# A new order of tiles, routing and quads, and up-projection weights of half 0 read from a ring that VectorE fills

## The reference

```python
x = x + _L0_conv_ref(_ln_c(x), conv_w_in, conv_w_out, conv_bin_weights)
t = _to_tokens(x)
t = t + _L0_ffn_ref(_ln_t(t), gate_w, gate_b, w1, w2, w3)
# _L0_ffn_ref: 16 experts, hidden width 128
logits = einsum('bsd,de->bse', x, gate_w) + gate_b
top_probs, top_idx = lax.top_k(softmax(logits), 2)
hidden = silu(einsum('bsd,edh->bseh', x, w1)) * einsum('bsd,edh->bseh', x, w2)
out = einsum('bseo,bse->bso', einsum('bseh,eho->bseo', hidden, w3), dispatch)
```

## Time and profile before

| | us |
|---|---|
| median of 3 runs | 467.33 (464.56 to 467.99) |
| the profiled execution | 460.52 |
| its span, first to last instruction | 458.7 |
| first sort of half 0 | 108.3 |
| first `up` of half 0 | 190.4 |
| last sort of half 1 | 263.3 |
| first `up` of half 1 | 309.0 |
| last `down` ends | 393.6 |

### The profile page before, as it was taken

One profiled execution on the slowest core, in us unless ns is written; L12 is line 12 of the kernel. 1 busy time (PEld: TensorE's weight loads), 2 busy tenths in 40 slices (PEclk: granted clock), 3 DMA queues, 4 the chain that ended last, 5 costly groups with the idle time before them and its releaser, 6 DMA issues.

```text
span 458.7 us, 8416 instructions
## 1 busy us (share of the span) xinstructions
PE 337.7 (74%) x2564; PEld 273.3 (60%) x2564; DVE 265.0 (58%) x576; ACT 224.3 (49%) x484; POOL 190.0 (41%) x165
## 2 busy tenths in 40 slices
PE   4676669854567743568887899978999999667665
PEld 4544448723455332457676797768778887555553
DVE  2958575879794576133333342203566662589995
ACT  4682745623567254444434444334555553256563
POOL 1187013402678235433333380007765400287770
PEclk9859785555555655555656669976999899555555
DMA  8999100000112104112222223342545432133321
GB/s 272 279 326 386 56 0 1 1 0 12 38 50 56 28 21 128 40 29 73 64 57 65 67 69 87 74 99 74 138 105 123 95 79 43 41 75 109 91 74 53
DMA packets 55388, 39.89 MB, mean 87 GB/s; under 512 B 37660, under 2 KB 49692, under 8 KB 54708
## 3 DMA queue, kind: packets, MB, share of 16 engines
q1 hardware_dynamic: 42804, 29.25, 22.5%
q0 software_dynamic: 12384, 10.10, 9.1%
q10 hardware_dynamic: 160, 0.01, 0.0%
HBM read 20.08 MB, written 19.14 MB: 85 GB/s over the span
## 4 chain that ended last, share of the span: by engine, by line
PE 49%; DVE 28%; issue 10%; ACT 6%; DMA 4%; POOL 2%; SPq 1%; DVEq 0%; ACTq 0%; POOLq 0%
PE banks L878 11%; PE banks L870 8%; PE banks L869 8%; PE banks L808 6%; PE banks L843 4%; DVE tok L1146 4%; DVE tok L1144 3%; DVE chosen L1210 2%; DVE cand L1204 2%; DMA xs<-sorted_y,back 2%; PE banks L891 2%; ACT xs L554 2%; PE banks L678 1%; ACT wcol L555 1%; DVE ct L966 1%
## 5 line engine op out<-in xcount | busy, mean ns | idle before, releaser
L1289 POOL DMA_INDIRECT sorted_x<-xs,addr x64 | 75.6, 1181 | 99.4 <-ACT xs L554 69.4
L1295 POOL DMA_INDIRECT xs<-sorted_y,back x64 | 75.0, 1172 | 97.1 <-issue 82.5
L1197 DVE SCALAR_TENSOR_TENSOR power<-banks,fold 128x512 f32<-128x512 f32 x46 | 31.8, 691 | 123.8 <-PE banks L870 107.9
L870 PE MATMUL banks<-shared,w_all 128*128 128x128 f16 x368 | 78.7, 255 | 0.0
L869 PE MATMUL banks<-shared,w_all 128*128 128x128 f16 x368 | 77.3, 255 | 0.1
L808 PE MATMUL banks<-shared,tok 128*76 128x131 f16 x256 | 40.0, 307 | 44.5 <-ACT wcol L555 25.1
L554 ACT CAST xs<-banks 76x512 f16<-76x512 f32 x64 | 37.2, 581 | 66.5 <-PE banks L808 66.1
L878 PE MATMUL banks<-w_all,power 128*128 x368 | 60.9, 318 | 4.6 <-ACT enh L593 2.1
L878 PEld LDWEIGHTS banks<-w_all,power 128*128 128x128 f32 x368 | 54.6, 228 | 10.2 <-issue 9.7
L808 PEld LDWEIGHTS banks<-shared,tok 128*76 128x76 f16 x256 | 27.4, 172 | 55.7 <-DVE tok L1146 40.4
L820 PE MATMUL banks<-ident,tok 128*76 128x128 f16 x256 | 40.3, 311 | 17.7 <-ACT w_raw L561 6.9
(11 more groups left out here) (175 smaller groups left out, 534.5 us busy)
## 6 DMA issues: line engine op xcount, KB each, us to landing
sorted_x<-zeros SPq DMA_DIRECT2D x2, 2944.0 KB, 30.8
w_raw<-sorted_x SPq DMA_DIRECT2D x22, 256.0 KB, 4.0
sorted_y<-filt SPq DMA_DIRECT2D x96, 32.0 KB
sorted_y<-enh SPq DMA_DIRECT2D x88, 32.0 KB, 1.8
w_raw<-in_L_ffn_w SPq DMA_DIRECT2D x5, 512.0 KB, 15.7
xs<-in_x SPq DMA_DIRECT2D x8, 256.0 KB, 5.3
out<-cen_sq SPq DMA_DIRECT2D x8, 256.0 KB, 2.7
shared<-in_t_fwd SPq DMA_DIRECT2D x1, 1024.0 KB, 8.0
```

The source lines that it names most:

```text
L870: last = nc.tensor.matmul(dst, of_expert(experts[(i % 2) * QUAD + b], a + 1, HID).bitcast(F16), tokens[:, b, :, :], start=False, stop=True)
L1289: nc.gpsimd.indirect_dma_start(out=sorted_x[k].rearrange("(g s) c -> g (s c)", s=GRP), out_offset=bass.IndirectOffsetOnAxis(ap=addr[:, k, ...
L1295: nc.gpsimd.indirect_dma_start(out=yl[m % YL_RING], out_offset=None, in_=sorted_y[k].rearrange("(g s) c -> g (s c)", s=GRP), in_offset=bas ...
```

## The change

Five edits go together.

1. On TensorE `places_for` is cut in three (`counts_for`, `ranks_for`, `places_for`), which for half 1 come at tiles 24, 27 and 29 instead of all at 26. VectorE does its part, `sort_places(1)`, after the last 0/1 matrix of half 0. `owners_of` is cut in `past_of` (tile 8) and the rest (tile 17); `owners_for(0)` comes at tile 8. ScalarE's `gap_exponential(1)` and the table load come after tile 24.
2. 4 tiles of half 1 are sorted up front instead of 8; the other 28 go into 19 quads instead of 24 into 12. Of a quad's tiles, one part is sorted between `up` and `down`, the other after the octet's transposes. VectorE writes the 0/1 matrices for quad q+1 ahead of `product(q)`.
3. The loop over quads is one loop over both halves: `down` of the last two quads of half 0 comes between the first `up`s of half 1. The transposes of an octet come after the `up` and `down` of the even quad before it.
4. In half 0 `up` reads its weights from a ring of four quads at fixed addresses. VectorE fills it two quads ahead with four copies a quad, 128x512 of 16 bits, whose source address is taken from a register. One extra matmul of 512 columns (`stay_warm`) stands ahead of each `up`. Half 1 and every `down` read through TensorE's registers as before.
5. The return of half 0 starts at quad 4 and takes 18 quads, instead of 3 and 16. `slot_weights(0)` moves into quad 2.

```diff
-OWNERS_AFTER, ROUTE_AFTER, PLACES_AFTER = 4, 14, 26
-UPFRONT, SORT_STEPS = 8, 12
+PAST_AFTER, OWNERS_AFTER, ROUTE_AFTER = 8, 17, 14
+COUNTS_AFTER, RANKS_AFTER, PLACES_AFTER = 24, 27, 29
+UPFRONT, SORT_STEPS = 4, 19
+FILLERS = 1
-RET_START, RET_STEPS, BACK_LAG = 3, 16, 3
+RET_START, RET_STEPS, BACK_LAG = 4, 18, 3
+FETCH_AHEAD, FETCH_RING = 2, 4
...
+            def up_weights(k, i, b, a, experts):
+                if k == 0:
+                    return fetched_w[:, (i % FETCH_RING) * QUAD + b, a * HID:(a + 1) * HID].bitcast(F16)
+                return of_expert(experts[(i % 2) * QUAD + b], a, HID).bitcast(F16)
+            def stay_warm(count, spare):
+                for _ in range(count):
+                    nc.tensor.matmul(spare, ident16[:, :], perm[:, 0:BLK], start=True, stop=True)
...
+                if k == 0:
+                    pe.wait_ge(fetched, q + 1)
...
+                    if a == 0 and k == 0:
+                        stay_warm(FILLERS, bank[first_bank + q % 2])
...
+            for q in range(HALVES * NQ + DOWN_LAG):
+                k, i = q // NQ, q % NQ
+                n = OCTETS * k + i // 2
+                first, second = halves_of(sorts_in(q))
+                if k < HALVES:
+                    up(k, i, experts[n])
+                for t in first:
+                    sort_tile(t)
+                if q >= DOWN_LAG:
+                    before = q - DOWN_LAG
+                    down(before, experts[OCTETS * (before // NQ) + before % NQ // 2])
+                if k < HALVES and i % 2 == 0 and n + 1 < HALVES * OCTETS:
+                    experts[n + 1] = owners(n + 1)
+                    transpose_tokens(n + 1)
+                for t in second:
+                    sort_tile(t)
...
+            def fetch(i):
+                o = i // 2
+                if i % 2 == 0:
+                    used = regs[o % 2][0:blocks_of(o)]
+                    nc.vector.load(used, owner[0:1, 0, o * OCT:o * OCT + len(used)])
+                    fetching[o] = [nc.vector.snap(r, min_val=0, max_val=E - 1) for r in used]
+                if i >= FETCH_RING:
+                    dve.wait_ge(h2_done, i - FETCH_RING + 1)
+                for b in range(QUAD):
+                    last = nc.vector.tensor_copy(fetched_w[:, (i % FETCH_RING) * QUAD + b, :],
+                                                 w_all[:, bass.ds(fetching[o][(i % 2) * QUAD + b], 1), 0:4 * HID].rearrange("p o n -> p (o n)"))
+                last.then_inc(fetched, 1)
...
+                    for n in sorts_in(q + 1):
+                        one_hots(n)
                     product(q)
                     if k == 0:
-                        for n in sorts_in(i):
-                            one_hots(n)
+                        if i + FETCH_AHEAD < NQ:
+                            fetch(i + FETCH_AHEAD)
+                        if i == 2:
+                            slot_weights(0)
```

More of the change, by code:

```diff
@@ L319, in build @@
         in_xg = [sem(f"in_xg{o}") for o in range(XG_RING)]
[L320 to L321 removed]
+        xt_ps, xt_done, h1_done, h2_done, silu_done, hid_done, y_ps, y_done, fetched = (
+            sem(n) for n in ("xt_ps", "xt_done", "h1_done", "h2_done", "silu_done", "hid_done", "y_ps", "y_done", "fetched"))
         y_stored = [sem(f"y_stored{r}") for r in range(YS_RING)]
@@ L358, in sorts_in, with halves_of @@
             left = HT - UPFRONT
-            return range(HT + UPFRONT + left * i // SORT_STEPS, HT + UPFRONT + left * (i + 1) // SORT_STEPS) if i < SORT_STEPS else ()
+            return range(HT + UPFRONT + left * i // SORT_STEPS, HT + UPFRONT + left * (i + 1) // SORT_STEPS) if i < SORT_STEPS else range(0)
+        def halves_of(tiles):
+            return tiles[0:len(tiles) // 2], tiles[len(tiles) // 2:]
         block = ctx.enter_context(nc.Block())
@@ L569, in _ @@
                 hott_out(t)
-                if t == PLACES_AFTER:
+                if t == COUNTS_AFTER:
                     gap_exponential(1)
@@ L606, in result @@
                                bank[OUT_BANKS[n % 2]].rearrange("p (k q x y) -> p k q x y", k=KT, q=2, y=16)).then_inc(res_done, 1)
[L608 to L617, removed]
-                        for n in sorts_in(i):
[L619 to L622, removed]
+            tokens_out(0)
+            for q in range(HALVES * NQ + DOWN_LAG):
+                k, i = q // NQ, q % NQ
+                first, second = halves_of(sorts_in(q))
+                if k < HALVES:
+                    gate(q)
+                for n in first:
+                    sorted_out(n)
+                if q >= DOWN_LAG:
+                    y_out(q - DOWN_LAG)
+                if k < HALVES and i % 2 == 0 and OCTETS * k + i // 2 + 1 < HALVES * OCTETS:
+                    tokens_out(OCTETS * k + i // 2 + 1)
+                for n in second:
+                    sorted_out(n)
+                if k == 1:
+                    for m in tiles_in(i, RET_START, RET_STEPS):
+                        high_part(m)
             for n in range(TURN):
@@ L759, in window, with counted, counts_for @@
                 return perm[:, at:at + count * HT]
-            def places_for(k):
+            misc = bank[MISC_BANK]
+            def counted(k):
+                return [groups[:, k, c:c + 1].to_broadcast([P, P]) for c in range(CHUNKS)]
+            def counts_for(k):
                 pe.wait_ge(chosen_done, k + 1)
@@ L773, in places_for, with ranks_for @@
                     nc.tensor.matmul(bank[0], below, chosen[:, k, j, :, :].rearrange("p e t -> p (e t)"), start=(j == 0), stop=False)
+            def ranks_for(k):
                 pe.wait_ge(groups_done, k + 1)
-                counted = [groups[:, k, c:c + 1].to_broadcast([P, P]) for c in range(CHUNKS)]
                 for c in range(CHUNKS):
@@ L1230, in return_end @@
                 add_tiles((HT * (k + 1)) // TURN - 1)
+            for i in range(FETCH_AHEAD):
+                fetch(i)
             for k in range(HALVES):
```

81 lines of the change are left out of this document (44 added, 37 removed).

## The result

| | before | after |
|---|---|---|
| median (us) | 465.94 (463.99 to 467.99) | 412.19 (410.25 to 415.43) |
| ratio | | 0.8853 [0.8779, 0.8926] |
| the profiled execution, its span | 460.52, 458.7 | 415.43, 413.4 |
| mean granted clock | 0.682 | 0.738 |

The account below looks back on a forecast made before the run. In half 0's sort quads no engine was full: short waits chained at a 0.59 clock. Savings of 15.0 (sort stage) and 28.9 (half 0), less 1.5 (half 1), made 42.4 off 460.5, or 418; forecast 421 us, range 405 to 446.

Parts of the forecast that it names:

- The sort stage: Before the first `up`: owners' wait gone, routing cut in three, fewer tiles up front; 15.0 us saved, `up` near 175.4.
- the table load: Sort stage: ScalarE's load of 1.28 us now stands between tiles that wait for ScalarE, costing about 1.1.
- What is late next: End of sort stage: the load of sorted slots starts near 168, lands near 172, just when TensorE needs it.
- The clock: Half 0: first four quads at the lower clock, 18.2 us, then the full clock with TensorE busy 3.2 of 3.7.
- VectorE's price: Half 0: VectorE needs 3.7 us a quad, copies 4 x 0.40 = 1.6 of it, and sets the pace at full clock.
- The range's lower end: Copies at 0.23 and a clock that rises at once: half 0 about 76, the time 404 to 411 us.
- The additions: End of half 0: GpSimd's eight additions fall beside the last copies and cost 4 us.
- one VectorE instruction among them took 2.80: Half 0's additions, seen in the profile before: they take 8.03 us, one VectorE instruction among them 2.80; 4 us allowed.
- The rival of copies behind GpSimd's scatters: Half 0: each copy waits about 1.0 us for GpSimd, 7.1 a quad, half 0 163, time 478 to 485; chance 0.04.
- Half 1: Keeps its registers; its 84.6 us grows by 1.5, since its first two quads now have a `down`; some 86.
- which its last gathers hide: Half 1: the return of half 0 is two steps later, and its last gathers were to hide that.
- The sum: Whole kernel: 15.0 + 28.9 - 1.5 = 42.4 us saved, 460.5 becomes 418; 421 forecast.

Follow-up runs that it names:

- the gathers apart: Against the kernel with GpSimd's additions behind the last copy: gathers two a quad from half 1's fifth quad, return one quad later; 397.91 us, ratio 0.8532.
- the late additions: Against the kernel after: GpSimd starts its eight additions only behind half 0's last VectorE copy; 403.88 us, ratio 0.8646; run again 408.44, 0.8715.

## Why the prediction was right, point by point

**The sort stage**, 15.0 forecast, 17.8 measured. Four of its mechanisms are in the rows: the owners without a wait, the routing as 6.2 us of TensorE's own work (1.1, 3.6 and 1.5 from the start of each piece, at 144.01, 150.55 and 156.19, to the next tile; the forecast had 6.5 ahead of the gaps that it fills), the table load (2.10 instead of 0.40: 1.7 where 1.1 was forecast), and VectorE late at the first tile of half 1 (2.50, forecast 3.2). What made up the 2.8 above the forecast was not taken apart; one part seen in the rows is the clock, which rose for some microseconds (1.04 instead of 1.91 for the same four matmuls).

**What is late next.** The slots' load went out at 165.42 and its transposes at 170.04 with 0.53 of idle time: in time, with nothing to spare, as forecast.

**The clock.** Right in kind and too cautious in size: forecast at the full clock from the fifth quad, 18.2 us for the first four; measured 11.0 (172.6 to 183.6), with the clock at full some 4 us behind the first `up`. The reason given, that the gaps of the sort's chain are loosened, is what the run without a ring bears out (15.0 us of waits for the sort before, none there). Which part of the new order did it was not told apart: the sorts between `up` and `down`, the matrices written ahead, or 28 tiles in 19 quads instead of 24 in 12. Against the forecast half 0 gained 7.2 by this term. One reading of the forecast's was wrong: the slice of 284 to 288, given as half 1, lies in half 0, in its quads without sorts; half 1 began at 309.0.

**VectorE's price**, 3.7 a quad forecast, 3.07 measured. The mis-sized term is the copies. A single one takes 0.286, where 0.30 was taken; but the four were summed as 4 x 0.40 = 1.6, and this row shows four in 0.90:

```profile
186.31 0.90 DVE L1258 COPY work<-w_all 128x512 uint16 x4
```

Each starts 0.20 behind the one before although it lasts 0.28, so they overlap, and the register arithmetic is hidden. That gives 0.7 a quad, about the whole difference. The range's lower end named this case ("copies at 0.23").

The Trainium skill, "VectorE: DVE Perf Modes", the tier table, gave an estimate of 0.30 for such a copy at four elements a cycle; the measured 0.286 agrees.

**The additions**, 4 us forecast as a last term of half 0; the last four quads took 22.0 (230.7 to 252.7) instead of 16. The step that failed is "one VectorE instruction among them took 2.80": the 2.80 was read as the whole price, but one copy waited for all eight additions, 8.42 here, `up` waited for the copy, and the clock fell behind it. Taken away, it gave 8.8.

The Trainium skill, "SBUF — State Buffer", Who interferes with whom, says that the loser is blocked for the whole of the other's instruction. The trace agrees that it is a block; it shows eight instructions where the rule speaks of one. It also says that an instruction with at most one input from SBUF, outside the two-port modes, does not contend, which agrees with the `product`s that kept their 0.69.

**The rival of copies behind GpSimd's scatters** did not come: scatters and copies shared the quads with sorts, and with the additions moved away no copy took over 0.635. Its time was added up wrongly: half 0 at 163 loses 44.4 and the rest gains 13.5, which gives 491 to 498 and not 478 to 485.

**Half 1**, 86 forecast and 93.4 measured. Nothing in the forecast saw the second hole; "which its last gathers hide" spoke of the return's end, not of its start. With the gathers apart half 1 took 89.4, with the late additions and the hole in place 92.1 and 94.4, so the hole is 3 to 5 of the 7; the late additions took another 1.3 in one of these runs, and the rest stays open.

**What follows the last `down`** was to stay and took 2.2 more. It varies from run to run without an edit there (65.0 to 70.8 us), and the kernel after has late signals of TensorE in it too (2.2 us at 382.90).

**The sum** gave a time 2.8 too high at the start and 9.6 in half 0, and 9.5 too low behind it. The mechanisms of the first two parts were right, but that the sum came within 3 us is luck: the errors have opposite signs.

## What to carry to other kernels

Read a stage's gaps before its busy shares: here the order, with the extra matmul in place, took away TensorE's short waits for the sort and brought 46 of 54 us and the full clock; the cheaper weight read brought 5 in the old order and 7 (16 without the additions beside the copies) in the new. Before a VectorE copy goes on the critical path, look for every GpSimd instruction it can meet, and put those where VectorE runs work that is not waited for; spreading them out did not help here, where VectorE was nearly full. Where a profile calls the end of a wait "remote", compare the semaphore's update with the row of the engine that gives it. Gathers issued in shorter runs went with 1.3 to 2.1% less time here, which is worth a try and no more than that.

## What the hardware showed that was not expected

- A 128x512 16-bit copy stood 8.42 us behind eight additions of about 1.0 each; small fp32 instructions got through one addition at a time (0.99 to 1.19 each), and 16-bit matrix instructions took up to 2.20 for 0.53 and 1.87 for 0.29 in the kernel with single additions between the scatters.
- Four such copies in a row take 0.90, not 4 x 0.286 = 1.14.
- In the old order the ring raised the granted clock of the sort quads from 0.59 to 0.71 (0.77 to 0.80 in most slices) with almost no gain in time.
- With runs of gathers of 1.13 at 1.44 apart, TensorE's signals came up to 4.8 us behind the modelled ends of its matmuls, and ScalarE waited 2 to 4 us for them; in the kernel before the same run of gathers had no late signal.
